# Low half of a split weight stacked under its high half: 17 passes for the down product of a tile instead of 18

## The reference

```
xz = x @ W_in; x_proj, z = split(xz)                  # 256 -> 2 x 512
x_conv = silu(causal_conv4(x_proj) + conv_b)
ssm = x_conv @ W_xproj                                # 33 columns: delta, B (16), C (16)
h_mean = einsum(x_conv, softplus(delta) * B) / L      # over the whole sequence
y = (C @ h_mean + D * x_conv) * silu(z)
x = layernorm(x + y @ W_out)

def fp4_linear(x, w): return fp4_quant_dequant(x) @ fp4_quant_dequant(w).T   # blocks of 16 in a row
h = silu(fp4_linear(x, w_gate)) * fp4_linear(x, w_up) # 256 -> 704
x = layernorm(x + fp4_linear(h, w_down))              # 704 -> 256
```

## Time and profile before

| | us |
|---|---|
| median of 3 runs | 2201.66 (2200.06 to 2202.36) |
| profiled execution, its own time | 2204.03 |
| span of the profile | 2202.1 |
| PE busy in it | 1990.6 (90%) |
| DVE busy | 1756.7 (80%) |
| GpSimd (POOL) busy | 1115.6 (51%) |
| ScalarE (ACT) busy | 1111.5 (50%) |

### The profile page before, as it was taken

The page is one execution under the profiler, slowest core; times in us unless marked ns, Lnnn a source line. Parts: engine busy times, 40 slices in busy tenths (PEclk is TensorE's granted clock), DMA queues, the critical chain, the costliest instruction groups (busy, mean ns, idle before and its releaser), DMA issues.

```text
span 2202.1 us, 37847 instructions
## 1 busy us (share of the span) xinstructions
PE 1990.6 (90%) x10532; PEld 1583.8 (72%) x10532; DVE 1756.7 (80%) x3548; ACT 1111.5 (50%) x2100; POOL 1115.6 (51%) x1643
## 2 busy tenths in 40 slices
PE   1887899899999999899999999899999999877776
PEld 1655688688877888688877888688876888666665
DVE  6234788798978888789877888798887888788875
ACT  2665455555545555455544556455544555423332
POOL 2223455466545556455644555465554556445543
PEclk9999999999999999999999999999999999999998
DMA  2111111111111111111111111111111111000000
GB/s 79 50 56 43 34 49 44 44 43 45 49 41 34 44 48 45 36 49 49 41 38 41 44 44 48 38 49 44 39 41 39 49 45 35 29 20 25 20 20 15
DMA packets 77089, 90.53 MB, mean 41 GB/s; under 512 B 8881, under 2 KB 59953, under 8 KB 76849
## 3 DMA queue, kind: packets, MB, share of 16 engines
q1 hardware_dynamic: 76848, 87.73, 12.2%
HBM read 37.37 MB, written 16.78 MB: 25 GB/s over the span
## 4 chain that ended last, share of the span: by engine, by line
PE 76%; issue 5%; DVE 4%; ACT 3%; POOL 1%; ACTq 0%; DVEq 0%; POOLq 0%
PE pgu L489 23%; PE pd L489 14%; PE pd L537 9%; PE pa L489 6%; PE pb L489 6%; PE pc L571 4%; PE pc L519 4%; PE pe_ L631 2%; PE pa L559 2%; PE pc L496 2%; PE pe_ L548 1%; PE pd L638 1%; DVE hbuf L990 1%; DVE qsh L820 1%; PE pa L615 1%
## 5 line engine op out<-in xcount | busy, mean ns | idle before, releaser
L489 PE MATMUL pgu<-wgu_hi,xqT 128*128 128x512 f32 (+1 forms) x1536 | 427.7, 387 | 0.9 <-issue 0.9
L489 PE MATMUL pd<-wd_hi,hqT 128*128 128x256 f32 (+1 forms) x1536 | 334.5, 299 | 18.7 <-DVE r L1012 15.5
L489 PEld LDWEIGHTS pgu<-wgu_hi,xqT 128*128 128x128 f32 x1536 | 279.8, 190 | 75.8 <-issue 27.6
L537 PE MATMUL pd<-wout,g 128*128 128x256 f32 x1024 | 259.9, 398 | 49.6 <-DVE hqT L980 35.2
L489 PEld LDWEIGHTS pd<-wd_hi,hqT 128*128 128x128 f32 (+1 forms) x1536 | 255.8, 190 | 57.4 <-issue 23.8
L946 DVE SCALAR_TENSOR_TENSOR acc<-xps,cw,acc 128x512 f32<-128x512 f32 x256 | 248.7, 972 | 24.4 <-POOL acc L429 23.7
L418 POOL TENSOR_SCALAR rs<-mv 128x1 f32<-128x1 f32 x128 | 61.6, 481 | 396.4 <-DVE mv L1027 228.8
L537 PEld LDWEIGHTS pd<-wout,g 128*128 128x128 f32 x1024 | 191.5, 195 | 79.7 <-issue 56.0
L741 ACT ACTIVATE hqT<-pe_ 128x512 fp32r<-128x512 f32 x128 | 76.2, 595 | 335.3 <-PE pe_ L631 335.3
L402 POOL TENSOR_TENSOR xv<-xnq,qsx 128x256 f32<-128x256 bf16 x128 | 79.5, 621 | 300.1 <-DVE xnq L839 300.1
L489 PE MATMUL pgu<-wgu_lo,xqT 128*128 128x512 f32 (+1 forms) x768 | 228.3, 379 | 0.0
(11 more groups left out here) (132 smaller groups left out, 4669.2 us busy)
## 6 DMA issues: line engine op xcount, KB each, us to landing
xcr<-xcs SPq DMA_DIRECT2D x128, 256.0 KB, 2.3
xin<-in_L_attn_x_dram SPq DMA_DIRECT2D x32, 512.0 KB, 3.9
xres<-in_L_attn_x_dram SPq DMA_DIRECT2D x128, 128.0 KB, 2.1
out_dram<-outb SPq DMA_DIRECT2D x128, 128.0 KB, 1.7
szr<-in_L_attn_W_in_dram SPq DMA_DIRECT2D x1, 1024.0 KB, 7.4
szr<-in_L_ffn_w_down_dram SPq DMA_DIRECT2D x1, 704.0 KB, 8.6
szr<-in_L_ffn_w_gate_dram SPq DMA_DIRECT2D x1, 640.0 KB, 4.5
szr<-in_L_ffn_w_up_dram SPq DMA_DIRECT2D x1, 640.0 KB, 5.7
```

Of the source, the lines that this page charges most:

```text
L489: mm = pe.matmul(bank, lhsT, rhs, start=(m == 0), stop=(m == len(pairs) - 1))
L537: mm = pe.matmul(pd[:, 0:DM], g[:, (s + 1) % 2, c, j * P:(j + 1) * P], wout[:, c, :], start=(c == 0), stop=(c == NB - 1))
```

## The change

The last 64 inner columns of h (block 5) are written twice into hbuf, at columns 640 to 703 and again at 704 to 767. After the transpose, rows 0 to 63 and 64 to 127 of the block are equal. The weights of block 5 hold the high part in rows 0 to 63 and the low part in rows 64 to 127. One pass over 128 rows then gives high times high plus high times low. The third pass, low times high, stays at 64 rows. So there are 17 passes a tile. The second copy is a GpSimd product of its own, put ahead of L432, with a wait of its own. The weights' last columns are doubled by four GpSimd copies before the last weight group; their low part is written by DVE into the upper rows in place. The memset of hbuf's last columns goes.

```diff
-        wd_lo = sb("wd_lo", [P, FC + 1, DM], F32R)
+        wd_lo = sb("wd_lo", [P, FC, DM], F32R)
...
+        twice_d = flat_xc[:, 5 * GW:5 * GW + KM * P]
...
+            pool.wait_ge(wq_ready, 3)
+            for h in range(KM):
+                rest = quant_w[2][:, h * FF + FC * P:(h + 1) * FF]
+                pool.tensor_copy(twice_d[:, h * P:h * P + FR], rest)
+                last = pool.tensor_copy(twice_d[:, h * P + FR:(h + 1) * P], rest)
+            last.then_inc(wq_ready, 1)
...
                     if exists(tg):
                         pool.wait_ge(hq_link, 6 * tg + 6)
+                        at_least(pool, hq_pe, 2 * tg)
+                        pool.tensor_tensor(blocks(hbuf[:, 2 * FF:FF + (FC + 1) * P]), blocks(hnq[:, FC * P:FF]),
+                                           spread(qsh[:, 1, FC * P // QB:QH]), ALU.mult)
                         pool.tensor_tensor(blocks(hbuf[:, FF:2 * FF]), blocks(hnq[:, :]),
                                            spread(qsh[:, 1, :]), ALU.mult).then_inc(hprod_done, 1)
...
-            for c in range(FC + 1):
-                m = P if c < FC else FR
-                pieces = [(quant_w[2][:, h * FF + c * P:h * FF + c * P + m], P) for h in range(KM)]
-                groups.append((m, pieces, wd_hi[0:m, c, :], wd_lo[0:m, c, :]))
+            for c in range(FC):
+                pieces = [(quant_w[2][:, h * FF + c * P:h * FF + (c + 1) * P], P) for h in range(KM)]
+                groups.append((P, pieces, wd_hi[:, c, :], wd_lo[:, c, :]))
+
+            pieces = [(twice_d[:, h * P:(h + 1) * P], P) for h in range(KM)]
+            groups.append((P, pieces, wd_hi[:, FC, :], None))
...
-        W_NEEDS = [1] * 4 + [2] * 4 + [3] * (FC + 1)
+        W_NEEDS = [1] * 4 + [2] * 4 + [3] * FC + [4]
...
-                for c in range(FC + 1):
-                    m_ = P if c < FC else FR
-                    pairs += [(hqT[0:m_, c, :], wd_hi[0:m_, c, :]),
-                              (hqT[0:m_, c, :], wd_lo[0:m_, c, :]),
-                              (hqT[0:m_, FC + 1 + c, :], wd_hi[0:m_, c, :])]
+                for c in range(FC):
+                    pairs += [(hqT[:, c, :], wd_hi[:, c, :]),
+                              (hqT[:, c, :], wd_lo[:, c, :]),
+                              (hqT[:, FC + 1 + c, :], wd_hi[:, c, :])]
+
+                pairs += [(hqT[:, FC, :], wd_hi[:, FC, :]),
+                          (hqT[0:FR, 2 * FC + 1, :], wd_hi[0:FR, FC, :])]
...
-            dve.memset(hbuf[:, 2 * FF:FF + (FC + 1) * P], 0.0).then_inc(w_zero, 1)
             dve.wait_ge(gu_landed, 16 * 4)
-            dve.wait_ge(w_zero, 3)
+            dve.wait_ge(w_zero, 2)
...
+                if lo is None:
+                    dve.tensor_tensor(hi[FR:P, :], (pa, pb)[n % 2][FR:P, 0:DM], hi[FR:P, :], ALU.subtract)\
+                        .then_inc(wt_lo, 1)
+                    continue
```

## The result

| | us |
|---|---|
| before, on the same chip | 2202.16 (2200.06 to 2205.87, 5 runs) |
| after | 2214.46 (2211.89 to 2216.82, 5 runs) |
| ratio | 1.0055 (95%: 1.0041 to 1.0070) |
| profiled execution after, its own time; span | 2216.82; 2215.0 |

The account below looks back on a forecast made before the run. PE was taken as the bound, with GpSimd close behind and body j=1 bound by DVE and GpSimd. Terms +1.6 + 5.0 - 0.6 - 3.3 + 0 - 1.9 gave +0.8 us: 2202.4, range 2189 to 2210.

Parts of the forecast that it names:

- d: Delay of GpSimd's large product L432 by the added small product: 0.24 us per tile, bounds 0.18 and 0.31.
- tight L631: PE's transpose of h close behind GpSimd's product in 49 tiles: net +0.06 us each, +1.6 in the 28 bodies j=3.
- body j=1: PE's transposes of xv wait for DVE and GpSimd; the delay passes on, the pass brings nothing: +5.0 us, or 0.
- The pass of body j=2: PE's transpose of h has 3.7 us of room there, so the removed pass counts fully: -3.3 us.
- The doubled weights at the start: Four GpSimd copies of w_down's last columns, some 1.2 us, hidden before the last weight group; otherwise +1.2 once.
- three signs: Wrong if L631 shows no idle time, the small product is far from 0.29 us, or L548's wait in j=1 shrinks.
- PE busy 15 us less: Expected in the profile after: PE's busy time falls by 15 us.
- step (3): Body j=0, PE's state projection: 0.36 us late, mostly covered by room and absorption; -0.6 us, bounds -3.3 and +1.4.
- steps (1) to (4): The terms for bodies j=3, j=1, j=0 and j=2, in that order: +1.6, +5.0, -0.6 and -3.3 us.
- The removed memset ...: nothing: At the start, dropping the memset of hbuf's last columns was claimed to change no time.
- The tail: The last 16 tiles, where the down product is on the chain: each pass counts, -1.9 us.
- rival "slower": Same mechanism with a small product costing 0.31 us or more, or its wait not hidden: +6.2 us, 2208; chance 0.28.

Follow-up runs that it names:

- e2: Kernel before plus GpSimd's small 128x64 product and its wait, still 18 passes; 2214.54 us beside 2202.28.
- e3: Changed kernel without GpSimd's small product and with DVE's memset back: 17 passes, one term left out; 2194.77 us, ratio 0.9966.
- e1: Changed kernel plus a one-column DVE memset of a spare tile ahead of its loop; 2210.65 us beside 2202.28.
- e7: e1 with ScalarE doing xcs ahead of xbig in body j=0; 2193.01 us beside 2203.31.
- e11: Kernel before with only ScalarE's xcs put ahead of xbig in body j=0; 2201.57 us, ratio 0.9992.
- e6: Kernel before with the memset of hbuf's last columns moved from DVE to GpSimd; 2206.41 us, ratio 1.0012.
- e5: Changed kernel with ScalarE making the second copy instead of GpSimd's product, and DVE's memset back; 2193.51 us beside 2203.31.
- e8: e5 plus xcs ahead of xbig on ScalarE in j=0 and xnq ahead of h on DVE in j=1; 2171.36 us, ratio 0.9854.
- e9: Kernel before, 18 passes, with xcs ahead of xbig (ScalarE, j=0) and xnq ahead of h (DVE, j=1); 2195.72 us beside 2203.93.
- e4: Changed kernel with GpSimd's small product behind the large one, with its own semaphore; 2216.88 us, ratio 1.0064.
- e10: e1 plus xcs ahead of xbig (ScalarE, j=0) and xnq ahead of h (DVE, j=1); 2188.85 us, ratio 0.9934.

## Why the prediction was wrong

**Right.** The size of d (0.25, predicted 0.24). The tight L631: 49 tiles wait, and a pass of PE and d of GpSimd make +0.06 where -0.12 was meant (0.00 and the shifted 0.06 in the table). The estimate of 0.20 us for the product, from the Trainium skill's figures (GPSIMD Engine Reference, section 3.1), was too low here: 298 ns were measured. In body j=1 the overlap carries d on: L836 on xv, now L850, takes 0.83 instead of 0.59, and the idle time ahead of the transposes of xv grows from 0.56 to 0.75 (DVE, then PE's load):

```profile
1046.51 0.83 DVE L850 SCALAR_TENSOR_TENSOR xv<-xbig,xv 128x256 f32<-128x256 f32 x1
...
1049.38 0.20 PEld L560 LDWEIGHTS pe_<-ident,xv 128*128 128x128 f32 x2 [0.75 <-issue]
```

The pass of body j=2 counts. The doubled weights at the start are hidden: GpSimd's four copies end at 43.75 us and PE loads the last weight group at 52.66. None of the three signs by which I had said that I would be wrong came; of the other signs, "PE busy 15 us less" did not come (2.4 less).

**Wrong, step (3), the room ahead of PE's state projection.** "d + 0.119 = 0.36 late, less 0.16 of room and 0.1 to 0.2 absorbed: 0 to 0.1 back", with xcs ending "0.21 us ahead of PE's state projection". The mechanism stood there: L830 longer by d, then xbig, xcs, PE. The room did not. 0.21 us is what the waits between xcs and that load take when PE is already waiting for them: in after xcs ends at 1032.62 + 0.62 = 1033.24 and the load follows at 1033.44, 0.20 behind, in a body in which it is the last thing waited for. The same distance stands in before, ScalarE and PE's load:

```profile
1025.06 0.61 ACT L760 ACTIVATE xcs<-acc 128x512 f32<-128x512 f32 x1
...
1025.88 0.73 PEld L571 LDWEIGHTS pc<-wxp,xcs 128*128 128x128 f32 x5
```

In the steady bodies j=0 it is 0.20 to 0.21 in before, e2, e3 and after alike (0.24 in one body of e1), while the load's idle time grows from 0.09 over 0.21 (e3) and 0.32 (e2) to 0.45; only where xcs is really early, in e7 to e11, is it longer (0.54) and the idle time 0.04. So I had read a path without slack as one with 0.16. The load stands for 0.45, and of d + 0.119 = 0.36 some 0.3 are lost in each such body, where I had put 0 to 0.1. The four windows sum to +0.34 in place of the +0.10 of my steps (1) to (4). e7 (0.30 back) and e11 (nothing to get back) show that it is this place.

**Wrong, "The removed memset ...: nothing".** As work it is nothing. But DVE's loop begins one instruction earlier, and one body in sixteen pauses, at some 1.1 us a batch (6.7 over six). e1 and e6 show that the place of that instruction makes the pause, in both directions; rows show what 0.35 us turn into. Why DVE pauses stays open. A transfer of the instruction queue stands 0.64 to 0.95 us behind L1029 in these bodies; but one stands 0.35 behind it in the same body of before and 0.46 in e1, where there is no pause, so it proves nothing. No row of before shows the pause. But the trace of before does show how little a lateness there must be to cost much: in this body GpSimd's L418 starts only 0.07 ahead of DVE's L836.

**Smaller.** The tail gave -0.6, not -1.9. The edges are not settled: they moved by -17 to +8 us over six batches between these kernels, and I cannot say why. Part of it may be the scatter that the trace of before shows in itself.

**The accounts**, for spans: steady middle batches without the pause +5.5 where my steps give about +2.0 for the same windows; the pause +6.7; edges -0.4; first 16 tiles +1.6 where I had 0.7; last 16 -0.6 where I had -1.9. Sum 12.8, measured 12.9. The rival "slower" had the sign, but not the mechanism: d was not dearer, what hung on it was.

## What to carry to other kernels

When a step adds work to a shared helper engine, ask for every place where the result ends just ahead of PE whether the distance is slack or the cost of the waits: take the same distance in a body where PE is seen waiting, and only what is beyond it is room. A pass removed from the bound engine counts in full only where no other engine follows closely: alone it gave 7.5 of 15.2 us (e3). Paid for by the engine that follows closely it cost 8.4 (e1); paid for by one with real slack (ScalarE here, 0.31 us a tile) it kept its gain (e5). Then look at which instruction stands needlessly ahead of the one PE waits for. Two reorderings gave another 22 us on top of e5 (e8), though only 8 on the kernel before (e9), and a good part of the 22 is at the edges, unexplained.

## What the runs showed of the hardware

- One DVE instruction more or fewer ahead of a long unrolled loop moved a pause of 0.35 us (134 or 487 ns between PE's last pass and the residual) in and out of one body per batch: it is there in after, e4 and e6, and not in before, e1, e2, e3, e5, e8, e9 and e11. In e7 (three of six batches) and e10 (all six) the same body has 267 to 291 ns.
- Who starts first on DVE and GpSimd matters at 0.04 us: a one-column GpSimd instruction took 0.22 us when it started 0.07 ahead of a 704-column DVE instruction with two SBUF inputs, and 0.93 when 0.04 behind, ending 0.08 behind the DVE instruction (e6). The Trainium skill (SBUF — State Buffer, section "SBUF: two separate sides") says that whichever of the two starts first has the shared pair for its whole length. For the GpSimd instruction the traces agree; DVE's took 0.89 in either order, so the other half does not show here.
- A GpSimd product of 128x64 took 298 ns on average ahead of the large one, and 484 ns on average behind it (e4; 0.74 us in the body shown).
- ScalarE copied 64 rows of 128 columns to the other 64 partitions in 0.31 us (e8, among its neighbours):

```profile
1002.31 0.76 ACT L793 ACTIVATE tap<-xps,cw 128x512 f32<-128x512 f32 x1
1003.09 0.31 ACT L798 ACTIVATE hqT<-hqT 64x128 fp32r<-64x128 f32 x1
```
